# The masked product of C and B stays in its PSUM bank: a Mamba-2 style layer on one Trainium2 core

## The chip, the cores and the metric

The kernel runs on one core of one Trainium2 chip. The metric is the device time of one execution in microseconds (us); lower is better. Names of the engines: PE is TensorE (its weight loads are listed as PEld), DVE is VectorE, ACT is ScalarE, POOL is GpSimd, SP is SyncE.

## What is computed

One layer over 2048 tokens of width 1024: a layer norm, then the sum of the input, a state space mixer (64 heads of 64 channels, 8 groups, state size 128) and a small feed-forward product with routed low-rank parts. The part that matters here is the scan of the mixer. The reference does it token by token:

```python
def step(state, inp):
    dA_t, dtx_t, B_t, C_t = inp
    state = state * dA_t[..., None, None] + dtx_t[..., None] * B_t[:, :, None, :]
    y_t = jnp.einsum('bhpn,bhn->bhp', state, C_t)
    return (state, y_t)
```

The kernel does it by chunks of 128 tokens. Within a chunk, with M the causal mask, it needs for each of the 8 heads of a group the 128 x 128 matrix (decay of the head between two tokens) x (C times B, masked by M), and multiplies that with the chunk's inputs.

## The kernel before, in words

The 2048 tokens are four blocks of 512 (a loop on the device over `q`). In a block the 8 groups of heads follow each other: group 0, a loop over three pairs of groups (1 and 2, 3 and 4, 5 and 6), and group 7. In a group the four chunks of 128 tokens run one after the other, and between their steps PE works through the dense units of the layer: 14 slots of weights a group (gate, x, B and C projections of the next group, output projection of the last). A weight of fp32 is split into a high and a low part (`w_hi` by ACT on line 501; `w_lo`, first half by POOL on line 362, second half by DVE on line 1020), and each product is three matmuls.

Every engine has its own list of instructions in an order written out by hand, and semaphores tie them together. Of one chunk, in the order of the program:

- PE (`chunk_1`) puts the chunk's x, transposed, into the bank `pX`; B, transposed, into columns 0 to 127 of the bank `pCB`; C times B into columns 128 to 255 of `pCB`.
- ACT (`chunk_1`) copies x out (`x_ck`, line 582) and B (`B_hi`, line 584), makes the decays in `E` (Relu on line 590, Exp on line 598, in two halves of four heads) and rounds `wx` (line 601).
- DVE (`chunk_1`, then `masked`) makes `dtx` and `wx` (lines 1136, 1137), the masked product `CBm` (line 1140), `B_lo` (line 1141), and then multiplies the two halves of `E`, 128 x 512 each, by `CBm` repeated for four heads (line 1148).
- POOL (`chunk_pre`, `wx_low`, `lo`, `inv_rms`) makes `xD`, `S_dec`, `C_lo`, `S_lo` (lines 400, 406, 413), `wx_lo` (line 418), weight halves in between, and the reciprocal root `rstd` (lines 424, 426).
- PE (`chunk_2`) multiplies C with the state into `pS` and `E` with `dtx` into `pY` (line 877); DVE (`chunk_2`) reads them (`y`, lines 1155, 1158, 1161). Only when DVE has read `pS` (line 1155) may PE (`chunk_2b`) write the new state's product into it. `chunk_3` transposes the normalized output into `pD0`, which DVE reads on line 1179 (`z_t`).

Between these steps DVE also does, for each x, B or C unit of the next group, the convolution: copies of three columns (lines 1108, 1110), three taps (line 1113) and the silu (line 1121); and ACT empties the unit's bank before them (lines 550, 551; for a gate unit lines 569, 570) and makes the tanh (line 557). PE may start a unit only when ACT or DVE has emptied the bank of the unit two before it. At a group's end DVE prepares the next group (`prep`, lines 1211 to 1221), for which ACT's first gate evacuation waits.

The bank `pCB` has 512 columns of fp32, of which 256 are in use in this stage.

Of the kernel before, what the change touches and what calls it, by code (L numbers as in the profile page):

```python
# [34 lines left out]
ALU = mybir.AluOpType  # L35
ACT = mybir.ActivationFunctionType

L, DM, H, P, N, G = 2048, 1024, 64, 64, 128, 8
# [5 lines left out]
Q = 128  # L44
# [38 lines left out]
def layer_kernel(nc, x_tok, x_tr, w_slots, group_const, dt_bias, a_log, d_skip, b_base, lora_b, out_tr):  # L83
    ctx = ExitStack()
    with ctx:
        def sb(name, shape, dt=F32):
            return ctx.enter_context(nc.sbuf_tensor(name, shape, dt))

        def pb(name):
            return ctx.enter_context(nc.psum_tensor(name, [128, 512], F32))  # L90

        def sem(name):
            return ctx.enter_context(nc.semaphore(name))
# [23 lines left out]
        C_hi, C_lo = sb("C_hi", [128, Q], F32R), sb("C_lo", [128, Q], F32R)  # L117
        S_hi, S_lo = sb("S_hi", [128, GC], F32R), sb("S_lo", [128, GC], F32R)
        wx_hi, wx_lo = sb("wx_hi", [128, GC], F32R), sb("wx_lo", [128, GC], F32R)
        CBm = sb("CBm", [128, Q])  # L120
        E = sb("E", [128, HPG, Q])
        dtx = sb("dtx", [128, GC])
        wx = sb("wx", [128, GC])
# [21 lines left out]
        causal = sb("causal", [128, 128])  # L145
# [33 lines left out]

        bank = [pb("dense0"), pb("dense1")]  # L180
        pX, pCB, pD0, pD1, pY, pS = pb("pX"), pb("pCB"), pb("pD0"), pb("pD1"), pb("pY"), pb("pS")
        ln_banks = [pCB, pX, pD1, pY]
        ln_banks_first = ln_banks + [pD0, pS] + bank

# [42 lines left out]
        cbm_done = sem("cbm_done")  # L227
        bl_done = sem("bl_done")
        m_done = sem("m_done")
# [40 lines left out]
        def chunk(q, g, c):  # L270
            return q * (G * NC) + g * NC + c
# [743 lines left out]
        def _(dve):  # L1015
# [57 lines left out]
            def heads(t):  # L1073
                return t.rearrange("t (h p) -> t h p", h=HPG)

            def per_head(kind, c):
                return tok_g[:, kind * NC + c, :].unsqueeze(2).broadcast_to([128, HPG, P])

            def block_body(q):
# [51 lines left out]
                def chunk_1(g, c):  # L1131
                    n = chunk(q, g, c)
                    if c == 0:
                        dve.wait_ge(prep_done, q * PREPS + g + 2)
                    dve.wait_ge(ck_evac, n * 2 + 1)
                    nc.vector.tensor_tensor(heads(dtx[:]), heads(x_ck[:]), per_head(0, c), ALU.mult).then_inc(xw_done, 1)  # L1136
                    nc.vector.tensor_tensor(heads(wx[:]), heads(x_ck[:]), per_head(1, c), ALU.mult).then_inc(xw_done, 1)  # L1137

                    dve.wait_ge(ck_evac, n * 2 + 2)
                    nc.vector.tensor_tensor(CBm[:], pCB[:, N:N + Q], causal[:], ALU.mult).then_inc(cbm_done, 1)  # L1140
                    nc.vector.tensor_tensor(B_lo[:], pCB[:, 0:N], B_hi[:].bitcast(F32), ALU.subtract).then_inc(bl_done, 1)
                    dve.wait_ge(cbm_done, n + 1)

                def masked(g, c):
                    n = chunk(q, g, c)
                    for h in range(2):
                        dve.wait_ge(exp_done, n * 2 + (h + 1))
                        nc.vector.tensor_tensor(E[:, 4 * h:4 * h + 4, :], E[:, 4 * h:4 * h + 4, :],  # L1148
                                                CBm[:].unsqueeze(1).broadcast_to([128, 4, Q]), ALU.mult).then_inc(m_done, 1)

                def chunk_2(g, c):

# [163 lines left out]
                def group(g, p, first=False, last=False):  # L1316
# [22 lines left out]
                    lo(g, k_gate(first, 0))  # L1339
                    lo(g, k_gate(first, 1))  # L1340
                    chunk_1(g, 0)
                    masked(g, 0)
                    lo(g, k_gate(first, 2))
                    if not first:
# [11 lines left out]
                    if first:  # L1356
                        router_top()
                    normalize(g, 0)
                    chunk_1(g, 1)
                    out_unit(1)  # L1360
                    masked(g, 1)
                    out_unit(2)

# [8 lines left out]
                    normalize(g, 1)  # L1372
                    gated_lo(g, 0)
                    chunk_1(g, 2)
                    masked(g, 2)

                    x = [2, 3] if first else [1, 2] if last else [0, 1]
# [158 lines left out]
```

## Time and profile before

| | us |
|---|---|
| median of 3 runs | 3534.68 (3530.49 to 3535.64) |
| span of the profiled execution | 3533.1 |
| PE busy | 3364.6 (95% of the span) |
| DVE busy | 3009.1 (85%) |
| ACT busy | 1925.7 (55%) |
| POOL busy | 1755.4 (50%) |

The span runs from the program's first instruction to its last; the profiled execution's own time is taken as its span plus what lies around it, some 1.6 us if it took the median. A busy time counts each moment once. Matmuls are pipelined and their ends are modelled, so that a busy PE is not a PE at its peak; what PE lost is read from its idle time, which stands in square brackets in a timeline with the work that ended it.

### The profile page before, as it was taken

To read this page: it belongs to the slowest core of one execution; us is meant where nothing else is said; L and a number is where in the kernel's file an instruction comes from. 1 tells how busy PE (TensorE), PEld (TensorE's weight loads), DVE (VectorE), ACT (ScalarE), POOL (GpSimd) and SP (SyncE) were. 2 spreads that over 40 slices of the span, in tenths; PEclk is the share of its full clock that TensorE was granted. 3 is DMA by queue.
4 is the path that set the end of the run, shared out by engine and by line. 5 is a ranking of instruction groups with operands and counts; after the bars stand their busy time and mean duration, and the time that the engine had idled before them with its cause. 6 is when DMAs were issued, how large, how long until landed. Compare 5 with 4: busy or idle time off the path is not lost.

```text
span 3533.1 us, 55385 instructions
## 1 busy us (share of the span) xinstructions
PE 3364.6 (95%) x16256; PEld 2784.1 (79%) x16256; DVE 3009.1 (85%) x4240; ACT 1925.7 (55%) x4198; POOL 1755.4 (50%) x1476
## 2 busy tenths in 40 slices
PE   7899999999989999999998999999999899999999
PEld 6788787788778788787877878877887787887877
DVE  6998888997699988889669998888967998988886
ACT  4555555663455555556346555556535555555563
POOL 3555454554354555545335545545434555554553
PEclk9999999999999999999999999999999999999999
DMA  4222222222422222223242222232324222232232
GB/s 141 86 97 98 97 97 93 98 97 101 146 84 90 102 93 99 97 96 114 84 150 86 96 91 100 92 102 96 108 96 139 90 96 91 96 96 96 101 103 102
DMA packets 97043, 356.69 MB, mean 101 GB/s; under 512 B 11200, under 2 KB 12352, under 8 KB 96192
## 3 DMA queue, kind: packets, MB, share of 16 engines
q1 hardware_dynamic: 74304, 268.20, 22.7%
q10 hardware_dynamic: 22400, 84.42, 6.9%
q8 instruction: 157, 2.57, 0.3%
q14 instruction: 182, 1.49, 0.1%
HBM read 343.67 MB, written 8.91 MB: 100 GB/s over the span
## 4 chain that ended last, share of the span: by engine, by line
PE 57%; DVE 21%; issue 12%; ACT 5%; POOL 3%; ACTq 1%; DVEq 0%; POOLq 0%
PE dense L794 16%; PE dense L796 15%; PE dense L795 15%; DVE conv_us L1113 6%; PE pY L877 4%; DVE w_lo L1020 2%; DVE xT L1121 2%; DVE dtx L1136 1%; DVE wx L1137 1%; ACT E L590 1%; ACT w_hi L501 1%; PE pS L794 1%; PE pS L796 1%; PE pS L795 1%; POOL w_lo L362 1%
## 5 line engine op out<-in xcount | busy, mean ns | idle before, releaser
L362 POOL TENSOR_TENSOR w_lo<-w_raw,w_hi 128x512 fp32r<-128x512 f32 x490 | 713.1, 1455 | 1217.2 <-ACT w_hi L501 1217.0
L794 PE MATMUL dense<-xn_hi,w_hi 128*128 128x512 f32 x2880 | 1161.4, 403 | 75.6 <-POOL w_lo L362 34.5
L796 PE MATMUL dense<-xn_hi,w_lo 128*128 128x512 f32 x2880 | 1132.8, 393 | 0.0
L795 PE MATMUL dense<-xn_lo,w_hi 128*128 128x512 f32 x2880 | 1132.6, 393 | 0.0
L501 ACT ACTIVATE w_hi<-w_raw 128x512 fp32r<-128x512 f32 x980 | 590.3, 630 | 831.3 <-PE dense L796 734.6
L794 PEld LDWEIGHTS dense<-xn_hi,w_hi 128*128 128x128 f32 x2880 | 549.3, 191 | 200.4 <-issue 55.0
L796 PEld LDWEIGHTS dense<-xn_hi,w_lo 128*128 128x128 f32 x2880 | 547.6, 190 | 119.1
L795 PEld LDWEIGHTS dense<-xn_lo,w_hi 128*128 128x128 f32 x2880 | 549.4, 191 | 110.1 <-issue 1.9
L1020 DVE TENSOR_TENSOR w_lo<-w_raw,w_hi 128x512 fp32r<-128x512 f32 x462 | 473.3, 1025 | 102.2 <-ACT w_hi L501 101.0
L1113 DVE SCALAR_TENSOR_TENSOR conv_us<-conv_in,const_g,conv_us 128x512 f32<-128x512 f32 x576 | 522.2, 907 | 13.6
L794 PE MATMUL dense<-z_hi,w_hi 128*128 128x512 f32 x1024 | 414.0, 404 | 12.8 <-DVE acc L1196 8.7
L796 PE MATMUL dense<-z_hi,w_lo 128*128 128x512 f32 x1024 | 401.4, 392 | 0.0
L795 PE MATMUL dense<-z_lo,w_hi 128*128 128x512 f32 x1024 | 399.7, 390 | 0.0
L1148 DVE TENSOR_TENSOR E<-E,CBm 128x512 f32<-128x512 f32 x256 | 347.6, 1397 | 40.6 <-ACT E L598 40.5
L590 ACT ACTIVATE E<-cum_b,tok_g 128x128 f32<-128x128 f32 x1024 | 314.7, 404 | 0.0
L557 ACT ACTIVATE conv_in<-conv_us 128x512 f32<-128x512 f32 x192 | 120.9, 630 | 333.2 <-DVE conv_us L1113 333.2
L1196 DVE TENSOR_TENSOR acc<-acc,dense 128x512 f32<-128x512 f32 x256 | 170.3, 683 | 149.1 <-PE dense L796 148.8
L877 PEld LDWEIGHTS pY<-dtx,E 128*128 128x128 f32 x2048 | 248.2, 191 | 11.2
L424 POOL TENSOR_TENSOR rstd<-ssq,eps_t 128x1 f32<-128x1 f32 x128 | 61.6, 481 | 375.6 <-ACT xD L612 375.6
L877 PE MATMUL pY<-dtx,E 128*128 128x64 f32 x2048 | 242.2, 271 | 0.0
L794 PEld LDWEIGHTS dense<-z_hi,w_hi 128*128 128x128 f32 x1024 | 192.6, 188 | 62.8 <-issue 26.8
L796 PEld LDWEIGHTS dense<-z_hi,w_lo 128*128 128x128 f32 x1024 | 192.3, 188 | 44.4
(173 smaller groups left out, 5035.8 us busy)
## 6 DMA issues: line engine op xcount, KB each, us to landing
w_raw<-w_slots_dram SPq DMA_DIRECT2D x490, 512.0 KB, 3.3
cum_b<-cum_scratch ACTq DMA_DIRECT2D x128, 512.0 KB, 3.6
acc<-x_tr_dram ACTq DMA_DIRECT2D x4, 2048.0 KB, 10.0
out_tr_dram<-acc ACTq DMA_DIRECT2D x16, 512.0 KB, 3.0
BC<-x_tok_dram SPq DMA_DIRECT2D x8, 512.0 KB, 3.3
conv_us<-x_tok_dram SPq DMA_DIRECT2D x8, 512.0 KB, 4.6
acc<-x_tok_dram SPq DMA_DIRECT2D x4, 512.0 KB, 5.2
lora_sb<-lora_b_dram SPq DMA_DIRECT2D x1, 512.0 KB, 7.2
```

What stands on the lines that cost most here:

```text
L362: nc.gpsimd.tensor_tensor(w_lo[s][:, 0:512], w_raw[s][:, 0:512], w_hi[s][:, 0:512].bitcast(F32), ALU.subtract).then_inc(lo0_done, 1)
L501: nc.scalar.activation(w_hi[s][:, sl], w_raw[s][:, sl], ACT.Copy).then_inc(hi_done, 1)
L557: nc.scalar.activation(conv_in[j % 2][:, 0:TB], conv_u[j % 2], ACT.Tanh).then_inc(tanh_done, 1)
L590: ins = nc.scalar.activation(E[:, h, :], cum_b[c % 2][:, h, :], ACT.Relu, scale=-1.0, bias=tok_g[:, 4 * NC + c, h:h + 1])
L794: nc.tensor.matmul(out, lhs[0], rhs[0], start=start, stop=False)
L795: nc.tensor.matmul(out, lhs[0], rhs[1], start=False, stop=False)
L796: return nc.tensor.matmul(out, lhs[1], rhs[0], start=False, stop=stop)
L877: mm = nc.tensor.matmul(pY[:, h * P:(h + 1) * P], E[:, h, :], dtx[:, h * P:(h + 1) * P], start=True, stop=True)
L1020: nc.vector.tensor_tensor(w_lo[s][:, 512:1024], w_raw[s][:, 512:1024], w_hi[s][:, 512:1024].bitcast(F32), ALU.subtract).then_inc(lo1_done, 1)
L1113: nc.vector.scalar_tensor_tensor(out=conv_u[r], in0=conv_in[r][:, t:t + TB], scalar=const_g[:, 4 * j + t:4 * j + t + 1], in1=conv_u[r], op ...
L1148: nc.vector.tensor_tensor(E[:, 4 * h:4 * h + 4, :], E[:, 4 * h:4 * h + 4, :], CBm[:].unsqueeze(1).broadcast_to([128, 4, Q]), ALU.mult).the ...
L1196: nc.vector.tensor_tensor(acc[:, i, :], acc[:, i, :], bank[b][:], ALU.add).then_inc(evac_dve, 1)
```

## The change

The tile `CBm` in SBUF goes. Its name now stands for columns 256 to 383 of the bank `pCB`, which nothing used in this stage. DVE writes the masked product there, and reads it there as the second factor of the multiplication with `E`. Shapes, types, waits and the order of all instructions stay as they are.

```diff
@@ -117,7 +117,6 @@
-        CBm = sb("CBm", [128, Q])
@@ -179,6 +178,7 @@
         pX, pCB, pD0, pD1, pY, pS = pb("pX"), pb("pCB"), pb("pD0"), pb("pD1"), pb("pY"), pb("pS")
+        CBm = pCB[:, N + Q:N + 2 * Q]
@@ -1137,7 +1137,7 @@
                     dve.wait_ge(ck_evac, n * 2 + 2)
-                    nc.vector.tensor_tensor(CBm[:], pCB[:, N:N + Q], causal[:], ALU.mult).then_inc(cbm_done, 1)
+                    nc.vector.tensor_tensor(CBm, pCB[:, N:N + Q], causal[:], ALU.mult).then_inc(cbm_done, 1)
                     nc.vector.tensor_tensor(B_lo[:], pCB[:, 0:N], B_hi[:].bitcast(F32), ALU.subtract).then_inc(bl_done, 1)
@@ -1146,7 +1146,7 @@
                         nc.vector.tensor_tensor(E[:, 4 * h:4 * h + 4, :], E[:, 4 * h:4 * h + 4, :],
-                                                CBm[:].unsqueeze(1).broadcast_to([128, 4, Q]), ALU.mult).then_inc(m_done, 1)
+                                                CBm.unsqueeze(1).broadcast_to([128, 4, Q]), ALU.mult).then_inc(m_done, 1)
```

On DVE, in the first chunk of group 0, the program's rows read so (out<-in; a minus is before, a plus is the change; what an instruction waits for stands behind it):

```order
 L1137 TENSOR_TENSOR wx<-x_ck,tok_g 128x512
 L1139 REGISTER_ALU
-L1140 TENSOR_TENSOR CBm<-pCB,causal 128x128 [waits ck_evac]
+L1140 TENSOR_TENSOR pCB<-pCB,causal 128x128 [waits ck_evac]
 L1141 TENSOR_TENSOR B_lo<-pCB,B_hi 128x128
 L1142 REGISTER_ALU
-L1148 TENSOR_TENSOR E<-E,CBm 128x512 [waits exp_done,cbm_done]
-L1148 TENSOR_TENSOR E<-E,CBm 128x512 [waits exp_done]
+L1148 TENSOR_TENSOR E<-E,pCB 128x512 [waits exp_done,cbm_done]
+L1148 TENSOR_TENSOR E<-E,pCB 128x512 [waits exp_done]
```

Nothing moved: the same rows in the same place with the same waits, one operand changed. The lists of PE, ACT, POOL and SP have no difference at all.

## Rows read from the trace of the kernel before

**Rows 1.** All waits of PE: who waited for whom, us in total, times, longest.

```profile
PE pS L794 <- DVE y L1155: 48.5, 40, 4.6
PE dense L794 <- POOL w_lo L362: 34.5, 8, 4.5
PE dense L794 <- ACT conv_us L570: 21.9, 32, 1.1
PE dense L794 <- ACT conv_us L551: 15.9, 16, 1.0
```

**Rows 2.** Windows (engine busy us, granted clock): chunks 1 to 3 of a group 0; of a group 6.

```profile
982.70:1048.00 65.30, 56.62 (x271) 47.28 (x270) 64.17 (x98) 38.93 (x86) 36.01 (x29) 0.92 0.21 73
1590.70:1643.50 52.80, 51.62 (x252) 42.83 (x251) 51.94 (x74) 31.46 (x68) 27.79 (x21) 1.00 0.26 90
```

**Rows 3.** Groups of DVE instructions by form (busy us, mean ns).

```profile
L1148 DVE TENSOR_TENSOR E<-E,CBm 128x512 f32<-128x512 f32 x256 | 347.6, 1397 | 40.6 <-ACT E L598 40.5
```

**Rows 4.** Single lines of DVE: durations in ns, shortest/median/longest.

```profile
L1148 DVE TENSOR_TENSOR E<-E,CBm x256: 675/1772/1828, 91.0 to 3473.2; 128x512 f32<-128x512 f32 x128
L1196 DVE TENSOR_TENSOR acc<-acc,dense x256: 672/687/691, 192.7 to 3528.4; 128x512 f32<-128x512 f32 x128
L1140 DVE TENSOR_TENSOR CBm<-pCB,causal x128: 276/278/281, 89.3 to 3471.0; 128x128 f32<-128x128 f32 x128
```

**Rows 5.** DVE timeline, third chunk of a group 6 (start us, us, what).

```profile
1595.02 3.51 DVE L1148 TENSOR_TENSOR E<-E,CBm 128x512 f32<-128x512 f32 x2
1598.45 1.78 DVE L1020 TENSOR_TENSOR w_lo<-w_raw,w_hi 128x512 fp32r<-128x512 f32 x1
1600.16 1.26 DVE L1108 COPY conv_in<-halo_in 128x3 f32<-128x3 f32 x1
...
1601.45 2.33 DVE L1113 SCALAR_TENSOR_TENSOR conv_us<-conv_in,const_g,conv_us 128x512 f32<-128x512 f32 x3
```

**Rows 6.** POOL timeline of the same stretch, and ACT's splits feeding it.

```profile
1594.99 1.29 POOL L413 TENSOR_TENSOR S_lo<-S_cur,S_hi 128x512 fp32r<-128x512 f32 x1
1596.25 1.74 POOL L362 TENSOR_TENSOR w_lo<-w_raw,w_hi 128x512 fp32r<-128x512 f32 x1
1597.95 1.74 POOL L418 TENSOR_TENSOR wx_lo<-wx,wx_hi 128x512 fp32r<-128x512 f32 x1
1599.65 1.74 POOL L362 TENSOR_TENSOR w_lo<-w_raw,w_hi 128x512 fp32r<-128x512 f32 x1
...
1595.48 1.15 ACT L501 ACTIVATE w_hi<-w_raw 128x512 fp32r<-128x512 f32 x2
...
1598.21 0.64 ACT L501 ACTIVATE w_hi<-w_raw 128x512 fp32r<-128x512 f32 x1 [0.44 <-PE dense L796]
```

**Rows 7.** PE timeline: idle at the end of that group 6, and of a group 4.

```profile
1637.53 0.49 PE L794 MATMUL dense<-xn_hi,w_hi 128*128 128x512 f32 x1 [1.00 <-ACT conv_us L551]
1645.15 0.49 PE L794 MATMUL dense<-xn_hi,w_hi 128*128 128x512 f32 x1 [1.13 <-ACT conv_us L570]
...
1436.22 0.79 PE L794 MATMUL dense<-xn_hi,w_hi 128*128 128x512 f32 x1 [4.11 <-POOL w_lo L362]
```

**Rows 8.** DVE timeline, chunk 3 of group 5; chunk 1 of group 6.

```profile
1522.31 1.28 DVE L1148 TENSOR_TENSOR E<-E,CBm 128x512 f32<-128x512 f32 x2
...
1576.28 2.38 DVE L1148 TENSOR_TENSOR E<-E,CBm 128x512 f32<-128x512 f32 x2
...
1580.24 0.69 DVE L1196 TENSOR_TENSOR acc<-acc,dense 128x512 f32<-128x512 f32 x1 [0.98 <-PE dense L796]
```

**Rows 9.** PE timeline: idle in the four chunks of a group 0.

```profile
977.82 0.50 PE L794 MATMUL pS<-wx_hi,B_hi 128*128 128x512 f32 x1 [1.96 <-DVE y L1155]
995.74 0.50 PE L794 MATMUL pS<-wx_hi,B_hi 128*128 128x512 f32 x1 [0.79 <-DVE y L1155]
1015.84 0.79 PE L794 MATMUL pS<-wx_hi,B_hi 128*128 128x512 f32 x1 [4.58 <-DVE y L1155]
```

**Rows 10.** PE timeline: idle in the first chunk of group 6.

```profile
1561.05 0.49 PE L794 MATMUL dense<-z_hi,w_hi 128*128 128x512 f32 x1 [0.26 <-ACT conv_us L570]
```

## The prediction

> **What bounds the kernel now.** I read the page first: PE is busy for 95% of the span, so anything won elsewhere counts only where PE waits. The list of PE's waits comes next. Apart from the start and the blocks' opening, its large entries are four [rows 1]: 48.5 us until DVE had read `pS` (line 1155), 34.5 us put down to a weight half of POOL, and 21.9 and 15.9 us until ACT had emptied a bank (lines 570 and 551). Then I laid PE's idle times along the groups, with the timelines.
>
> In group 0 of a block PE waits in every chunk for DVE's reading of `pS`, 1.96, 0.79, 4.58 us in the first three [rows 9]; the fourth is of the same kind. DVE is busy for 64.17 of 65.30 us over the last three chunks [rows 2]: here DVE is the bound. The mean granted clock of 0.92 there says that PE spent part of the stretch at the lower of its two levels (1.2 against 2.4 GHz) around these idle times.
>
> In the groups of the loop PE runs nearly without a break until the end of the group. There it loses 1.00 us before the next group's second gate unit and 1.13 us before its third, both until ACT had emptied a bank [rows 7]. The first kind occurs 16 times in the kernel and the second 32 times with a smaller sibling of 0.26 us [rows 1, 10]: 16 x 1.1 + 16 x 0.26 = 22. So 16 group ends are bound so: groups 1, 3, 5 and 6 of four blocks. ACT is only the messenger: its evacuations stand behind its tanh, and that behind DVE's taps; DVE is busy for 51.94 of the last 52.80 us of the group [rows 2]. Groups 2 and 4 end otherwise: 4.11 us of idle time, 8 times in all [rows 1, 7], where the pair loop jumps back. The weight half named there is inferred, and in a group 6 the same unit starts without it; only the jump differs. I take this as a fixed price that no earlier DVE shortens.
>
> **What the changed instruction costs now.** Line 1148 runs 256 times with a mean of 1397 ns [rows 3], but no single one takes 1397: they take 675 ns or some 1772 [rows 4]. (1397 - 675) x 256 = 185 us of excess, or 185 / 1.10 = 168 long ones. The timelines laid on each other show which. In the third chunk of a group 6 DVE needs 3.51 us for the pair while POOL works without a pause; the first ends at about 1596.8, just after POOL's `S_lo` ended at 1596.28, the second after POOL's `w_lo` [rows 5, 6]. In the last chunk of a group POOL is idle at that point and the pair takes 1.28 us [rows 8]. So DVE is held until the running POOL instruction ends, and POOL's own then shows 1.74 in place of 1.29 us [rows 6]: the two take turns.
>
> DVE's additions that read one operand from PSUM, `acc` (line 1196), never show this: 672 to 691 ns over 256 executions beside a POOL that is half busy [rows 4]. The Trainium skill states it as a rule (SBUF — State Buffer, "Who interferes with whom"): a DVE instruction with two SBUF inputs contends with a GpSimd one that reads SBUF and the second to issue is blocked until the first ends, while one with at most one SBUF input does not contend. The trace agrees, 1772 against 687 ns.
>
> After the change line 1148 has one input in SBUF and one in PSUM. Nearest rows: 672 to 691 ns for that form; what no row shows is a repeated read of 128 columns of PSUM. Bounds: 0.68 us, and 1.77 us, as if nothing were gained. I take 0.69, since the repeat in SBUF costs nothing either (675 ns). Line 1140 now writes PSUM in place of SBUF: 278 ns now [rows 4]; nothing shows the write, and I keep 0.28, bounded by the 0.28 of now and the 0.69 of four times as many columns. Busy time of DVE falls by some 185 us. That is not the gain.
>
> The skill has a rule against the change (VectorE: DVE Perf Modes, "The TRN2 errata"): a fixed part of 120 cycles for a PSUM source against 58, thus by estimate 65 ns more for each instruction. By it 4 instructions on the path of each of 16 group ends would give back 4 us in all. The rows show 687 against 675 ns, one fifth of that; the sum goes by the rows.
>
> **What of it reaches the path.** Each DVE instruction with two SBUF operands, and each three-column copy, takes its turn with POOL; if line 1148 leaves the queue, its followers meet POOL in its place. Third chunk of group 6, step by step [rows 5, 6]: the pair starts at 1595.02 and ends at about 1596.3. The weight half (line 1020) can start at 1596.65, when ACT's second split has ended (1595.48 + 1.15). POOL's `w_lo` runs from 1596.25, now unhindered, to 1597.5; DVE is held and ends at 1598.1 (0.54 behind POOL, as the first of the pair now is). `wx_lo` then runs to 1599.25, and holds the copy. The next `w_lo` runs to 1600.55 and holds the first tap, which now starts after it; the taps end at 1601.15 + 2 x 0.76 = 1602.7, against 1603.8. Before, four were held (two of line 1148, the half, the copy); after, three. **Shift of the chain: 1.1 us** of the 2.2 that the pair gets shorter.
>
> Nothing on this chain waits for PE until the group's end (DVE idles 0.86 us of 52.8), so the shift should arrive there. In the last chunk the pair is short already and gives nothing. PE's idle time that can go at such an end is 1.00 + 1.13 = 2.1 us, so the 1.1 passes.
>
> - 16 group ends x 1.1 us = 17.6 us.
> - The 8 ends of groups 2 and 4: only the short wait for `pS` ahead of the jump. The 48.5 us of rows 1 are 4 x 10.7 in the groups 0 and 24 times 0.2, so 8 x 0.2 = 1.6 us.
> - First chunk: the pair shortens by 2 us, and POOL's `wx_lo` holds a gate tile instead. About 1 us stays, which removes the 0.26 us before the output units [rows 10]: 16 x 0.26 = 4.2 us. PE's next wait, 0.5 us for `acc`, hangs on POOL's `rstd`, and that on an ACT split released by PE; it stays.
> - Second chunk: nothing. DVE waits 0.98 us for PE just behind the pair [rows 8], which is the cover; without it the pair's 1.1 us would count.
> - Group 0: the first chunk has the pair, the half and two gate tiles against the same POOL burst, 0.5 us; the second is as the worked one, 0.9 us. Third and fourth have short pairs, as in a group's last chunk. 4 x 1.4 = 5.6 us. What DVE owes in the third chunk, 4.58 us, is hardly touched.
> - Group 7: PE idles nowhere in its later chunks, 0.
>
> Sum 17.6 + 1.6 + 4.2 + 5.6 = 29 us. Against the profiled execution's 3533.1 us of span that is 3504.1, and with the 1.6 us around it the median of 3534.7 becomes **3506 us** (0.8% faster).
>
> **Rivals.**
> 1. *The turns are only passed on.* If the followers are held as long as line 1148 was, or ACT (its split waits for PE) or POOL's `rstd` sets the pace of the last chunk, the shift is about 0 and only a few 0.26 us waits go: within 7 us of before, 3528 to 3541. For it: one follower more is held in the working above, and half of the 2.2 us is gone at once. Against it: four became three, and POOL itself is 0.45 us faster for each turn saved.
> 2. *More passes than I count.* A shifted chain may meet POOL's second burst (last chunk) otherwise and shed one more turn. The cap is what PE idles: 16 x 2.1 + 1.6 + 4.2, and in group 0 the full 2.0 and 2.2 us of both pairs, 4 x 4.2. That is 56 us: 3479.
> 3. *The repeated PSUM read is slow* (the other side). Price p per instruction in all four chunks. Two pairs lie on the chain of a group end, the last of them short today, so the shift becomes 1.1 - 4 x (p - 0.68): zero at p = 0.95 us, and a loss beyond. At p = 1.77 the third chunk is as before and the last costs 2.2 us more: 16 x 2.2 + 4 x 4.4 (two short pairs in group 0) = 53 us slower, 3588. For it: no row reads PSUM with a repeat. Against it: no PSUM operand in any row of DVE costs more than some 15 ns.
>
> **How the numbers follow.** Forecast 0.70, with a shift of 0.5 to 1.7 us per group end: 8 + 7 = 15 to 27 + 15 = 42 us, so 3493 to 3520. Rival 1 0.13, rival 2 0.12, rival 3 0.05. The clock adds or takes some 2 us per block, since its low stretches stand beside PE's longer idle times (0.92 in the mean of group 0's stretch [rows 2]), and where PE idles less they may go. The range 3478 to 3524 holds the forecast and most of rival 2. A measurement of this kernel tells a change from none from about 0.2% (7 us): faster 0.82, within 0.13, slower 0.05.
>
> **What would show it.** Line 1148 at 675 to 700 ns in all 256, its busy time from 348 to about 175 us; line 1140 still near 280. Longer means for the followers: the weight half (line 1020), the taps, the gate tiles, so that DVE's busy time falls by clearly less than 185 us, some 90 to 120. POOL's busy time falls. PE's wait for line 551 falls from 1.0 us to near 0 at 16 ends, and the one for line 570 stays near 1.1; the 8 of 4.1 us stay. Group 0 keeps a wait of over 4 us in its third chunk. The forecast is wrong if line 1148 is above 0.95 us, or if it is short and those PE waits stand where they stood.

## The result, and the profile after

The changed kernel takes 3473.55 us (median of 4 runs, 3472.08 to 3474.9) against 3532.59 us before (4 runs, 3530.11 to 3535.64). The ratio is 0.9833, 95% interval 0.982 to 0.9845: 1.7% or 59 us faster. The forecast was 29 us. The direction was right, the forecast gain was half of what came, and the time lies 4.5 us below the range.

The first line and the busy times of the page after. The columns are busy time, share of the span, and number of instructions:

```profile
span 3472.5 us, 55385 instructions
...
PE 3347.7 (96%) x16256; PEld 2786.0 (80%) x16256; DVE 2799.0 (81%) x4240; ACT 1917.4 (55%) x4198; POOL 1670.7 (48%) x1476
```

Before, DVE was busy for 3009.1 us and POOL for 1755.4. DVE lost 210 us and POOL 85, and of that PE's span got back 60.6. The single lines that the change touches, in ns, shortest/median/longest [rows 4]; `rstd` (line 424) is POOL's and was not touched:

```profile
L1148 DVE TENSOR_TENSOR E<-E,pCB x256: 669/675/691, 90.2 to 3411.4; 128x512 f32<-128x512 f32 x128
L1140 DVE TENSOR_TENSOR pCB<-pCB,causal x128: 283/286/290, 88.4 to 3410.4; 128x128 f32<-128x128 f32 x128
L424 POOL TENSOR_TENSOR rstd<-ssq,eps_t x128: 189/189/677, 103.6 to 3429.7; 128x1 f32<-128x1 f32 x128
```

Line 1148 is short in all 256 executions, so the repeated read of 128 columns of PSUM costs nothing that shows (675 ns, as the shortest before). Line 1140, which now writes PSUM, costs 8 ns more. `rstd`, a single column, had 191/667/757 before.

DVE's groups by form, after (busy us, mean ns | idle before). The page of before had 522.2 us and 907 ns for line 1113, 473.3 and 1025 for line 1020, 116.3 and 929 for line 1128:

```profile
L1113 DVE SCALAR_TENSOR_TENSOR conv_us<-conv_in,const_g,conv_us 128x512 f32<-128x512 f32 x576 | 549.7, 954 | 13.6
L1020 DVE TENSOR_TENSOR w_lo<-w_raw,w_hi 128x512 fp32r<-128x512 f32 x462 | 441.3, 955 | 133.1 <-ACT w_hi L501 131.7
L1148 DVE TENSOR_TENSOR E<-E,pCB 128x512 f32<-128x512 f32 x256 | 163.2, 677 | 40.1 <-ACT E L598 40.1
L1128 DVE SCALAR_TENSOR_TENSOR gate<-conv_in,conv_us 128x512 f32<-128x512 f32 x128 | 96.2, 771 | 8.8 <-DVE z_t L1179 4.7 <-ACT conv_us L570 2.6
```

The pairs lost 184 us, as forecast. The taps (line 1113) took 27 us of it over, as forecast; but the weight halves (line 1020) and the gate tiles (line 1128) got shorter instead of longer, by 32 and 20 us.

The waits of PE after (us in total, times, longest), to be laid beside [rows 1]. The entry for `acc` was 11.7 us, 19 times, before, and there was no entry "issue":

```profile
PE pS L794 <- DVE y L1155: 34.4, 14, 4.4
PE dense L794 <- POOL w_lo L362: 24.7, 7, 3.7
PE dense L794 <- ACT conv_us L570: 17.9, 16, 1.1
...
PE dense L794 <- issue: 6.3, 2, 5.5
PE dense L794 <- ACT conv_us L551: 3.6, 16, 0.2
...
PE dense L794 <- DVE acc L1196: 2.1, 2, 1.1
```

Line 551 fell from 15.9 to 3.6 us. Of line 570's 32 waits the 16 of 0.26 are gone. So are 26 of the 40 waits for `pS`, and, against the forecast, 17 of the 19 waits for `acc`.

**The third chunk of group 6 again**, DVE's timeline after, for [rows 5]:

```profile
1566.52 1.27 DVE L1148 TENSOR_TENSOR E<-E,pCB 128x512 f32<-128x512 f32 x2
1568.15 1.44 DVE L1020 TENSOR_TENSOR w_lo<-w_raw,w_hi 128x512 fp32r<-128x512 f32 x1 [0.36 <-ACT w_hi L501]
1569.52 1.25 DVE L1108 COPY conv_in<-halo_in 128x3 f32<-128x3 f32 x1
1570.68 0.15 DVE L1110 COPY halo_out<-conv_in 128x3 f32<-128x3 f32 x1
1570.81 3.31 DVE L1113 SCALAR_TENSOR_TENSOR conv_us<-conv_in,const_g,conv_us 128x512 f32<-128x512 f32 x3
```

And POOL's, for [rows 6]:

```profile
1566.49 1.30 POOL L413 TENSOR_TENSOR S_lo<-S_cur,S_hi 128x512 fp32r<-128x512 f32 x1
1567.75 1.30 POOL L362 TENSOR_TENSOR w_lo<-w_raw,w_hi 128x512 fp32r<-128x512 f32 x1
1569.00 1.75 POOL L418 TENSOR_TENSOR wx_lo<-wx,wx_hi 128x512 fp32r<-128x512 f32 x1
1570.70 1.29 POOL L362 TENSOR_TENSOR w_lo<-w_raw,w_hi 128x512 fp32r<-128x512 f32 x1
```

This is the chain as worked out. The pair no longer holds POOL or is held (POOL's first two at 1.30), the weight half waits 0.36 us for ACT's split and is then held until 0.54 us behind POOL's `w_lo`, the copy is held by `wx_lo`, the first tap by the last `w_lo`. From the pair's start to the end of the taps it was 8.76 us (1595.02 to 1603.78) and is 7.60 (1566.52 to 1574.12): 1.16 us shorter, against 1.1.

PE at the end of that group, for [rows 7], with the back jump after group 2 as the third row:

```profile
1607.80 0.49 PE L794 MATMUL dense<-xn_hi,w_hi 128*128 128x512 f32 x1 [0.20 <-ACT conv_us L551]
1615.42 0.49 PE L794 MATMUL dense<-xn_hi,w_hi 128*128 128x512 f32 x1 [1.12 <-ACT conv_us L570]
...
1215.04 0.79 PE L794 MATMUL dense<-xn_hi,w_hi 128*128 128x512 f32 x1 [5.49 <-issue]
```

From the pair's start to the third gate unit after the group's end it was 1645.15 - 1595.02 = 50.13 us and is 1615.42 - 1566.52 = 48.90: 1.23 us, the shift of the chain. The first part of the group (third gate unit of its own to the pair of its third chunk) went from 1595.02 - 1546.71 = 48.31 to 1566.52 - 1519.47 = 47.05: another 1.26 us, where the forecast had 0.26. Here lies most of the gain that the forecast missed.

### The profile page after: what moved, and what is told of

Its sections match the earlier page's. It is cut to its first block, busy times and chain, and to the rows that moved or that the text cites. A ratio compares the mean times of both kernels' runs of the same rounds, so it can differ in the third digit from the quotient of the medians.

```text
span 3472.5 us, 55385 instructions
## 1 busy us (share of the span) xinstructions
PE 3347.7 (96%) x16256; PEld 2786.0 (80%) x16256; DVE 2799.0 (81%) x4240; ACT 1917.4 (55%) x4198; POOL 1670.7 (48%) x1476
## 4 chain that ended last, share of the span: by engine, by line
PE 61%; DVE 20%; issue 11%; ACT 3%; POOL 2%; ACTq 0%; DVEq 0%; POOLq 0%
PE dense L794 17%; PE dense L796 17%; PE dense L795 17%; DVE conv_us L1113 7%; PE pY L877 4%; DVE xT L1121 2%; DVE w_lo L1020 2%; DVE conv_in L1108 1%; ACT w_hi L501 1%; PE pS L794 1%; PE pS L796 1%; PE pD L895 1%; PE pS L795 1%; PE pX L862 1%; POOL w_lo L362 1%
## 5 line engine op out<-in xcount | busy, mean ns | idle before, releaser
L362 POOL TENSOR_TENSOR w_lo<-w_raw,w_hi 128x512 fp32r<-128x512 f32 x490 | 658.4, 1344 | 1222.2 <-ACT w_hi L501 1220.7
L794 PE MATMUL dense<-xn_hi,w_hi 128*128 128x512 f32 x2880 | 1161.7, 403 | 58.8 <-POOL w_lo L362 24.7
L1113 DVE SCALAR_TENSOR_TENSOR conv_us<-conv_in,const_g,conv_us 128x512 f32<-128x512 f32 x576 | 549.7, 954 | 13.6
L1020 DVE TENSOR_TENSOR w_lo<-w_raw,w_hi 128x512 fp32r<-128x512 f32 x462 | 441.3, 955 | 133.1 <-ACT w_hi L501 131.7
L424 POOL TENSOR_TENSOR rstd<-ssq,eps_t 128x1 f32<-128x1 f32 x128 | 38.2, 299 | 394.5 <-ACT xD L612 394.5
L795 PEld LDWEIGHTS dense<-z_lo,w_hi 128*128 128x128 f32 x1024 | 192.9, 188 | 37.1
```

Source lines behind the costliest of these rows:

```text
L362: nc.gpsimd.tensor_tensor(w_lo[s][:, 0:512], w_raw[s][:, 0:512], w_hi[s][:, 0:512].bitcast(F32), ALU.subtract).then_inc(lo0_done, 1)
L794: nc.tensor.matmul(out, lhs[0], rhs[0], start=start, stop=False)
L795: nc.tensor.matmul(out, lhs[0], rhs[1], start=False, stop=False)
L1020: nc.vector.tensor_tensor(w_lo[s][:, 512:1024], w_raw[s][:, 512:1024], w_hi[s][:, 512:1024].bitcast(F32), ALU.subtract).then_inc(lo1_done, 1)
L1113: nc.vector.scalar_tensor_tensor(out=conv_u[r], in0=conv_in[r][:, t:t + TB], scalar=const_g[:, 4 * j + t:4 * j + t + 1], in1=conv_u[r], op ...
```

## The experiments

In the first four the masked product stands in the bank for one chunk of a group only, and in `CBm` in SBUF for the rest; in their rows line numbers are one higher. The edit, here for chunk 0:

```diff
+        CB_of = [pCB[:, N + Q:N + 2 * Q] if c in (0,) else CBm[:] for c in range(NC)]
-                    nc.vector.tensor_tensor(CBm[:], pCB[:, N:N + Q], causal[:], ALU.mult).then_inc(cbm_done, 1)
+                    nc.vector.tensor_tensor(CB_of[c], pCB[:, N:N + Q], causal[:], ALU.mult).then_inc(cbm_done, 1)
-                                                CBm[:].unsqueeze(1).broadcast_to([128, 4, Q]), ALU.mult).then_inc(m_done, 1)
+                                                CB_of[c].unsqueeze(1).broadcast_to([128, 4, Q]), ALU.mult).then_inc(m_done, 1)
```

**First chunk only.**

> Only the first chunk of each group keeps the masked product in PSUM; the other three keep the SBUF tile. My theory after the result: the first chunk carries both the 0.55 us per group before the first output unit (16 times) and the wait for acc before the second output half (0.8 us in 16 groups, 0.3 us in 12), because the whole DVE and ACT sequence of the first chunk moves, 25 us in all, plus about 0.5 us in each group 0: 24 to 30 us faster. The theory of the prediction (acc wait tied to POOL's rstd and an ACT split released by PE, it stays): 4 to 11 us faster, with PE's waits for acc still at 19.

Measured 3514.96 us against 3532.0, ratio 0.9954 (0.9937 to 0.997): 17 us faster. That is four times the prediction's 4.2, and below the 24 to 30 expected here. PE's waits:

```profile
...
PE dense L795 <- POOL w_lo L363: 34.4, 8, 4.5
PE dense L795 <- ACT conv_us L571: 17.9, 16, 1.1
PE dense L795 <- ACT conv_us L552: 16.0, 16, 1.0
...
PE dense L795 <- DVE acc L1197: 2.2, 2, 1.2
```

The waits of the group's end stand where they stood (16 for line 551, here L552, and the 16 long ones for line 570), and 17 of the 19 for `acc` are gone. The step "it stays" is refuted by the one edit that it was about.

**Second chunk only.**

> Only the second chunk of each group in PSUM. Both theories: DVE waits for PE right behind this pair, so nothing in the groups of the loop; 0.9 us in each group 0: 3 to 5 us faster, within what can be told from nothing. A rival, that every freed turn of DVE helps, wherever it stands: 60/4 = 15 us.

3533.18 us against 3532.0, ratio 1.0005 (0.9996 to 1.0015): no change. The cover of 0.98 us [rows 8] holds. Even group 0's 0.9 us per block, 3.6 in all, isn't seen, and the rival that every freed turn helps (15 us) is out.

**Third chunk only.**

> Only the third chunk in PSUM. Theory: it alone feeds the DVE chain that ends a group. 16 ends x 1.24 us (the 0.46 us wait for pS goes and 0.78 of the 1.16 us wait for line 551) = 20 us, and 8 x 0.46 = 4 us before the back jump: 20 to 27 us faster; waits for line 570 before the third gate unit unchanged at 1.37 us. If the chain shortens only together with the other chunks, well under 15 us.

3505.67 us against 3532.0, ratio 0.9931 (0.9914 to 0.9948): 26 us faster. PE's waits:

```profile
PE pS L795 <- DVE y L1156: 41.7, 16, 4.4
PE dense L795 <- POOL w_lo L363: 25.6, 7, 3.8
PE dense L795 <- ACT conv_us L571: 21.9, 32, 1.1
PE dense L795 <- DVE acc L1197: 10.8, 18, 1.2
...
PE dense L795 <- ACT conv_us L552: 4.3, 16, 0.3
```

This is the mirror image: the end's wait for line 551 (here L552) falls to 4.3 us, the 24 short ones for `pS` go, and the first chunk's waits (L571 32 times, `acc` 18 times) stay. The idle time at the eight back jumps gets 3.6 us shorter (34.5 to 25.6, plus one of 5.2 under "issue").

**Fourth chunk only.**

> Only the last chunk in PSUM. Its pair is short already (677 to 682 ns) in all groups but the four last ones of a block. Theory: no change, within 3 us of before. It also prices the PSUM operand by itself on a chain that DVE bounds: if a PSUM write or a PSUM read cost more than SBUF, this kernel would be slower by 20 x 2 x the difference; 10 ns each give 0.4 us, 300 ns would give 12 us.

3529.14 us against 3532.0, ratio 0.9994 (0.9984 to 1.0004): no change. The pair is short there before and after, so this is the price of the PSUM operand alone: none that can be measured. (Of the 40 waits for `pS` 15 are left, 41.0 us in place of 48.5. That is no gain of this size: the 24 short ones of 0.17 to 0.22 us are 0.10 to 0.14 us now, and the profile shows idle time only from 0.15 us on. Between the starts of the matmuls they got 0.06 us shorter each, 1.5 us in all.)

**First and third chunk together** (`c in (0, 2)`).

> The first and third chunk of each group in PSUM, the second and last in SBUF. If the parts simply add, 17 + 26 = 43 us faster than before (3489). If the two together free more than each alone, as the sum of the four single runs (45 us) against the whole change (59 us) may hint, 50 to 59 us faster (3473 to 3482), and the second and last chunk then are worth nothing.

3481.96 us against 3531.15, ratio 0.9867 (0.985 to 0.9883): 49 us faster, against 17 + 26 = 43 for the two singly and 59 for all four. By the intervals the two together gave 41 to 53 us, the first alone 11 to 22 and the third alone 18 to 30, so that a surplus over their sum is not shown. All four gave 55 to 64, which is clear of 41 to 53: the second and the last chunk, worth nothing alone, are worth something with the others. The four times lie at 3477, 3478, 3486 and 3488 us, and the profile is of the shortest, so that it explains only part of the difference. It shows the second chunk's pair long in all 64 executions, where it was long in 44 before (in the run of the first chunk alone it is 64 too): there the turns were passed on. Outside group 0 that costs nothing, as the run of the second chunk showed. In the four groups 0, where DVE is the bound, PE gained 1.1 us in this run and 7.1 with all four chunks changed.

**Is it POOL that makes the pair long?** The kernel before, with the collision partner of the first, third and fourth pair taken out: POOL's `S_lo` covers one column, the rest is zero. That leaves out part of a low-order product.

```diff
-                        ins = nc.gpsimd.tensor_tensor(lo_part[:], raw, hi_part[:].bitcast(F32), ALU.subtract)
+                        w = 128 if lo_part is C_lo else 1
+                        ins = nc.gpsimd.tensor_tensor(lo_part[:, 0:w], raw[:, 0:w], hi_part[:, 0:w].bitcast(F32), ALU.subtract)
```

> The kernel before, with the masked product in SBUF, but POOL's S_lo (128x512) is done for one column only and the rest of S_lo is zero: this part of the low-order product is left out. If what holds line 1148 is whichever POOL instruction runs then, the pairs of the first and third chunk become short (near 0.68 us each) although both inputs stay in SBUF, and the kernel gains as much as with the operand in PSUM: 45 to 65 us. If line 1148 is slow beside POOL for another reason (its SBUF operand with a repeat, say), the pairs stay near 1.77 us and the gain is under 10 us.

3427.79 us against 3535.67, ratio 0.9696 (0.9679 to 0.9713): 108 us faster, about twice the gain expected. The pair, still with both factors in SBUF (line numbers two higher):

```profile
L1150 DVE TENSOR_TENSOR E<-E,CBm x256: 674/686/1790, 92.4 to 3367.7; 128x512 f32<-128x512 f32 x128
```

It is short in the first, third and fourth chunk, and long in 56 of 64 executions in the second, where other POOL work runs. So it isn't the operand in SBUF that is slow; a POOL instruction beside it makes it so. The edit takes more away than the pairs' partner: `S_lo` takes 0.30 us in place of 1.46, so that all of POOL's work behind it can start sooner, and the mean of `wx` falls from 1158 to 919 ns. The gain beyond 59 us can come from there; no run separates it.

**The same edit on the changed kernel.**

> The changed kernel with POOL's S_lo cut to one column as in the run e5 (the rest of that low-order part is left out). If the change works only by taking line 1148 out of the turns with POOL, it is worth little where S_lo is short already: in e5 only the pairs of the second chunk were still long, and that chunk alone was worth nothing outside group 0. So within 10 us of the 3428 us of e5. If the PSUM operand gives something by itself, another 40 to 60 us below e5.

3422.39 us against 3531.15, ratio 0.97 (0.9687 to 0.9714): 109 us faster than before, as the kernel without the change was (108). Once `S_lo` isn't there, the change is worth nothing that these ratios tell (0.9696 without it, 0.97 with it), though PE still waited 9.2 us for line 570 and 27.9 for `pS` in the run before, so that there was something left to win. What the change brings it brings through the turns with POOL; another way is not seen.

**The same medicine for the next two.** The changed kernel, with `dtx` and `wx` reading their x factor from the bank `pX`, where it still stands, in place of its copy in SBUF:

```diff
-                    nc.vector.tensor_tensor(heads(dtx[:]), heads(x_ck[:]), per_head(0, c), ALU.mult).then_inc(xw_done, 1)
-                    nc.vector.tensor_tensor(heads(wx[:]), heads(x_ck[:]), per_head(1, c), ALU.mult).then_inc(xw_done, 1)
+                    nc.vector.tensor_tensor(heads(dtx[:]), heads(pX[:]), per_head(0, c), ALU.mult).then_inc(xw_done, 1)
+                    nc.vector.tensor_tensor(heads(wx[:]), heads(pX[:]), per_head(1, c), ALU.mult).then_inc(xw_done, 1)
```

> The changed kernel, and in addition dtx and wx (lines 1137 and 1138) read x from the bank pX, which holds the same numbers, in place of the SBUF copy. Turn-taking theory: both fall from 1.15 us to 0.68 us in all 128, held instructions drop by most of 148, followers take over a part again; what PE still loses to DVE is 16 x (0.4 + 1.4) us at group ends and 45 us in the groups 0: 15 to 40 us faster than the change. Rival, that the rest of PE's waits come from ACT: under 5 us faster.

3423.53 us against 3535.67, ratio 0.9686 (0.967 to 0.9702); 50 us below the changed kernel. DVE's groups; the means were 1157 and 1124 ns:

```profile
L1136 DVE TENSOR_TENSOR dtx<-pX,tok_g 128x512 f32<-128x512 f32 x128 | 87.2, 681 | 13.2 <-ACT x_ck L582 13.2
L1137 DVE TENSOR_TENSOR wx<-pX,tok_g 128x512 f32<-128x512 f32 x128 | 86.6, 677 | 0.0
```

The wait for line 551 has gone and that for line 570 fell from 17.9 to 4.0 us. That the end's second wait was DVE's lateness too, with ACT as the messenger, is thereby shown. So is a thing that the prediction had excluded: at the eight back jumps, too, PE waits less when DVE is earlier.

```profile
PE dense L794 <- POOL w_lo L362: 17.7, 8, 2.4
```

```profile
1389.79 0.49 PE L794 MATMUL dense<-xn_hi,w_hi 128*128 128x512 f32 x1 [2.22 <-POOL w_lo L362]
```

```profile
350.00:354.00 4.00, 3.90 (x17) 3.26 (x18) 3.96 (x9) 2.51 (x5) 1.23 (x2) 1.00 0.23 61
```

These eight took 34.5 us before, 24.7 + 5.5 after the change, and 17.7 now, 2.1 to 2.4 each. Moreover the granted clock, which was 0.50 to 0.63 in the 4 us behind all eight before and after the change, is 1.00 behind seven of them here (the third row is such a window: us, busy time of PE, PEld, DVE, ACT, POOL with the number of instructions, granted clock, DMA; the eighth shows 0.63). Compared matmul by matmul with the changed kernel, the ends with a back jump gained 27.0 us and the 16 others 22.2.

**The back jump.** The changed kernel, with PE's loop over the pairs of groups written out (the other engines keep theirs):

```diff
-                with pe.Fori(0, 3) as pair:
+                for pair in range(3):
```

> The changed kernel, with PE's loop over the three pairs of groups written out; all other engines keep their loop. If the idle time at the 8 group ends (3 to 5.5 us) is the price of PE's own jump back, it goes, and the ends look like the others (1.75 us): 8 x (4.2 - 1.4) + what the low clock behind it costs, 8 x 1.7: 20 to 40 us faster than the change. If it comes from another engine's jump or from a late weight half of POOL, nothing changes.

3446.32 us against 3535.67, ratio 0.9753 (0.9737 to 0.977); 27 us below the changed kernel. PE's waits, and the end of the group 2 that had 5.49 us:

```profile
PE dense L794 <- ACT conv_us L570: 30.3, 24, 1.7
...
PE dense L794 <- ACT conv_us L551: 5.8, 24, 0.3
```

```profile
1216.00 0.49 PE L794 MATMUL dense<-xn_hi,w_hi 128*128 128x512 f32 x1 [1.68 <-ACT conv_us L570]
```

No entry is put down to POOL's `w_lo` any more, and "issue" has 0.9 us in all: the eight ends wait for lines 551 and 570 as the other sixteen do, 24 in all. Since only the loop was changed, POOL's name on that wait was a wrong label, and the wait needs the jump to appear. But it was not the jump's price alone: some 1.8 us of it came back at each of these ends as waits for lines 551 and 570, the wait for a late DVE that the longer one had covered. Idle time fell by 31.0 + 21.5 - 36.1 = 16 us. The rest fits the clock. Windows of the changed kernel around that jump (us; busy PE, PEld, DVE, ACT, POOL; granted clock; DMA):

```profile
1205.00:1215.00 10.00, 4.55 (x21) 3.42 (x19) 9.82 (x17) 5.37 (x10) 1.51 (x1) 0.85 0.19 56
1215.00:1219.00 4.00, 3.96 (x10) 3.16 (x11) 3.93 (x9) 1.33 (x4) 1.74 (x2) 0.51 0.37 135
1219.00:1223.00 4.00, 4.00 (x19) 3.29 (x18) 1.72 (x8) 1.00 (x2) 1.29 (x1) 1.00 0.02 6
```

After an idle time of 5.49 us PE runs at the lower of its two levels, 1.2 GHz (0.51), for 4 us and gets through 10 matmuls, where the 4 us after them, at full clock, see 19: 9 matmuls of 0.23 us each, 2 us on top of the 5.5. The 4 us behind the other seven jumps had 9 to 12 matmuls at a granted clock of 0.50 to 0.63. Written out, the stretch shows 1.00. Some 1.7 us at eight places are 14 us by estimate; with the 16 of idle time that is 30, and compared matmul by matmul these eight ends got 29.7 us shorter (the openings of the blocks took some of it back). The Trainium skill warns of such jumps (Runtime: NRT & Kernel Launch, "Instruction fetch mechanics"): a taken branch to code outside the fetched pages stalls the engine until the code is fetched. It gives no number; the runs agree in sign, and price the jump at 27 / 8 = 3.4 us each, clock included, as long as DVE is as late as here. That the time goes into fetching code is not shown by any of them.

**Both edits on the changed kernel.**

> The changed kernel with both: x read from pX, and PE's loop written out. If they are independent, the sum of the two gains, 35 to 80 us below the change (3395 to 3440 us).

3410.57 us against 3535.67, ratio 0.9651 (0.9635 to 0.9667): 122 us or 3.5% faster than before the change, 63 us below it. This is the best version with the full computation. The sum of the two is 77. They share the eight ends: compared matmul by matmul, the earlier DVE alone gained 27.0 us there and the written-out loop alone 29.7, both together 40.8. With DVE early, writing the loop out brings only 13 us more (3423.53 to 3410.57), 1.6 us for each jump. The 3.4 us above hold a late DVE and the low clock behind the long wait as well.

## Why the prediction was half right

PE's matmuls are the same and in the same order in all kernels here. So the start of every matmul can be subtracted from its start before the change, and the growth of that lag says where PE's time was gained. By stretches, in us, of the profiled executions (a stretch ends at the pair of a chunk; the end of a group runs from its third chunk's pair to the next group's first):

| stretch | times | priced | all four chunks | first alone | third alone | first and third |
|---|---|---|---|---|---|---|
| ends of groups 1, 3, 5, 6 | 16 | 17.6 | 19.6 | 0.1 | 19.0 | 18.8 |
| first to third chunk, groups 2, 4, 6, 7 | 16 | 4.2 | 19.5 | 19.7 | 0.1 | 19.7 |
| first to third chunk, groups 1, 3, 5 | 12 | 0 | 2.5 | 2.7 | 0.3 | 2.7 |
| ends of groups 2, 4 (back jump) | 8 | 1.6 | 9.3 | 3.5 | 10.8 | 12.8 |
| group 0 | 4 | 5.6 | 7.1 | -2.7 | 0.1 | 1.1 |
| group 7's end and block openings | 4 | 0 | 2.6 | -4.2 | -0.2 | 2.3 |
| sum | | 29 | 60.6 | 19.1 | 30.2 | 57.5 |

The first three rows repeat from run to run within 1 us. The last three don't add up from chunk to chunk, and no run tells why.

**What bounds the kernel: right.** PE ends the span and waits, at the group's end, for DVE through ACT. The third chunk alone moved line 551's wait, `dtx` and `wx` moved line 570's. Only the ends of groups 2 and 4, set apart as a fixed price, were bound so as well.

**The price of the instruction: right.** 675 ns against the 0.69 us taken; 0.286 us against 0.28 for line 1140. The 65 ns more for a PSUM source, an estimate from the Trainium skill (VectorE: DVE Perf Modes, "The TRN2 errata"), aren't seen here: 669 to 691 ns, and 3529.14 us with the fourth chunk alone.

**Followers take the turns: half right.** In the worked chain it came out row for row. But over the kernel DVE's busy time fell by 210 us and not by 90 to 120. I counted what the change hands on and not what it ends: an earlier DVE finds POOL idle in other places (weight halves -32 us, gate tiles -20). The executions of DVE that were held (over 0.2 us longer than the shortest of their line and form) fell from 879 to 725. The 168 of line 1148 went, and all other lines together have 14 more: the taps 98 to 127, `wx` 76 to 60.

**16 group ends x 1.1 = 17.6: right.** 19.6 us, 1.22 each, and the third chunk alone brought them.

**First chunk, 16 x 0.26 = 4.2: the step that failed.** The prediction put it so: PE's next wait "hangs on POOL's `rstd`, and that on an ACT split released by PE; it stays". It went, and the first chunk alone brought 17 us. In groups 2, 4, 6 and 7 of the four blocks the first part of a group got 1.22 us shorter (1.15 to 1.27), 19.5 us in all; in the twelve groups 1, 3 and 5 0.2 each, 2.5 us. The step priced 4.2. Two errors sit in it.

The first is the chain. In the timelines of DVE and POOL before, ahead of that `acc` wait, `rstd` is itself held:

```profile
1568.14 0.68 DVE L1020 TENSOR_TENSOR w_lo<-w_raw,w_hi 128x512 fp32r<-128x512 f32 x1
...
1569.53 1.26 DVE L1166 TENSOR_SCALAR yn<-y,rstd 128x512 f32<-128x512 f32 x1
```

```profile
1568.18 0.69 POOL L424 TENSOR_TENSOR rstd<-ssq,eps_t 128x1 f32<-128x1 f32 x1 [1.70 <-ACT xD L612]
```

And after:

```profile
1539.82 0.68 DVE L1020 TENSOR_TENSOR w_lo<-w_raw,w_hi 128x512 fp32r<-128x512 f32 x1
...
1541.30 1.26 DVE L1166 TENSOR_SCALAR yn<-y,rstd 128x512 f32<-128x512 f32 x1 [0.19 <-POOL rstd L426]
```

```profile
1540.45 0.19 POOL L424 TENSOR_TENSOR rstd<-ssq,eps_t 128x1 f32<-128x1 f32 x1 [2.06 <-ACT xD L612]
```

Before, a late weight half of DVE starts 0.04 us ahead of the one-column `rstd` and holds it until its own end; `rstd` takes 0.69 us and `yn`, which needs it, comes late. After, DVE is early, the half is almost over when `rstd` comes, and it takes 0.19 us. Turns are taken in both directions, and I had followed only POOL holding DVE. `yn` starts 1.35 us after the start of `rstd` before and 0.85 after. Another 0.27 us comes from `wx` (line 1137) in the second chunk, which took 0.95 us beside POOL's `C_lo` and takes 0.68 after. That the wait depends on the first chunk's pair is shown (that edit alone removes it, the third chunk's doesn't). That it works through `rstd` and `wx` is argued from the rows; no run held either alone. The places fit. Before, the first chunk's `rstd` takes 0.68 to 0.71 us in the 16 groups in which the `acc` wait of 0.55 stands, 0.40 to 0.43 in the groups 1, 3 and 5, which gained 0.2, and 0.19 in group 0. With the first chunk alone it takes 0.19 in all 32 and the waits are gone; with the third alone it is held in 28 again and they stand. `wx` of the second chunk is held in 16 of 32, and in none where the first chunk is changed.

The second error is that I took idle time for loss. PE before, at the `acc` wait:

```profile
1573.39 0.40 PE L796 MATMUL dense<-z_hi,w_lo 128*128 128x512 f32 x1
1574.34 0.50 PE L794 MATMUL dense<-z_hi,w_hi 128*128 128x512 f32 x1 [0.55 <-DVE acc L1196]
```

Matmuls that follow each other start every 0.22 or 0.23 us, though each is drawn with 0.39. Here 1574.34 - 1573.39 = 0.95 us lie between two starts, so 0.72 are lost where 0.55 are shown. In the same way more than 0.26 us is lost at the wait of [rows 10]. Set against the changed kernel, PE's lag grows by 0.47 us at that wait and by 0.78 at this one, 1.25 together, the gain of the stretch. The prediction priced 0.26.

**The 8 back jumps: priced 1.6, worth 9.3; a second step that failed.** The prediction took this wait as "a fixed price that no earlier DVE shortens". It isn't fixed. In the mean of the eight places it was 4.3 us before, 3.8 after the change, 2.4 with `S_lo` cut short and 2.2 with x read from `pX`. So the jump and the lateness of DVE both go into it. Of the 9.3 us, 4.4 are that idle time (34.5 to 24.7 + 5.5). The short `pS` waits ahead of it were worth 0.46 us each between starts where 0.19 was shown, 3.6 us in all. Why one of the eight got longer (5.49) and the others 3.2 to 3.7, no run tells.

**Group 0: 5.6 priced, about 7 measured.** The four waits of block 1 after, for [rows 9] (the fourth was 3.32 before):

```profile
961.68 0.50 PE L794 MATMUL pS<-wx_hi,B_hi 128*128 128x512 f32 x1 [1.30 <-DVE y L1155]
978.51 0.50 PE L794 MATMUL pS<-wx_hi,B_hi 128*128 128x512 f32 x1 [1.29 <-DVE y L1155]
998.43 0.79 PE L794 MATMUL pS<-wx_hi,B_hi 128*128 128x512 f32 x1 [4.40 <-DVE y L1155]
1018.58 0.50 PE L794 MATMUL pS<-wx_hi,B_hi 128*128 128x512 f32 x1 [2.09 <-DVE y L1155]
```

The third keeps over 4 us, as forecast. The matmul behind the fourth takes 0.50 us in place of 0.73. That the sizes agree doesn't confirm the working behind the 5.6, half a microsecond from the first chunk and 0.9 from the second of each block: alone, the first lost 2.7 us there.

Rival 2 gave 56 us, and so was right in size, but by another way: it let the ends shed 2.1 us each, and they shed 1.22; the rest came from the first chunk and the back jumps. That its size fits is luck. Rivals 1 and 3 are out: the turns were not merely passed on (154 held executions fewer), and the repeated read is not slow.

## What to carry to other kernels

Where a DVE instruction of one form shows two durations, 675 and 1772 ns here, look at what POOL runs beside it before looking at the instruction: an operand left in its PSUM bank takes it out of the queue for turns, and idle columns of a bank can hold an operand that DVE itself made. Follow the turns in both directions and over the whole loop, since an engine that comes earlier also stops holding the other one. Price a wait of PE by the distance between matmul starts and not by the idle time shown. Test a wait that stands only at a loop's back jump by writing the loop out, and don't take it for fixed: 4.3 us of it became 2.2 here when another engine came earlier.

## What the hardware showed beside that

- One POOL column can be held until a DVE instruction of 512 columns ends: `rstd`, 128x1, took 0.69 us beside DVE's weight half and 189 ns when that had almost ended.
- PSUM as destination of DVE costs next to nothing: 286 against 278 ns for 128 columns; as a repeated source nothing (675 ns in the median, and 675 ns in the shortest with both inputs in SBUF).
- A jump back on PE showed 3.2 to 5.5 us of idle time after the change, and the granted clock was 0.50 to 0.63 in the 4 us behind all eight. With x read from `pX` it showed 2.1 to 2.4 us, and the clock stayed at 1.00 behind seven of eight. With no jump the place of the 5.49 shows 1.68 us, and a clock of 1.00.
